# Attention and expert layer on one core: ten instead of eight tiles of the shared expert in the output stage

## What is computed

```python
gate = xt @ Wr + br
_, ids = top_k(gate + gate_bias, 2)            # 2 of 7 experts for each row
probs = softmax(masked)                        # over the chosen two
u = xt @ Wup[e] + bup[e]
g = silu(u @ Wgate[e] + bgate[e]) * u
eo = g @ Wdown[e] + bdown[e]
out = sum over the two experts of probs * eo
su = xt @ Wsu + bsu                            # the shared expert, for every row
sg = silu(su @ Wsg + bsg) * su
out = out + sg @ Wsd + bsd
```

## Time and profile of the kernel before

| | |
|---|---|
| median of three runs | 996.62 us |
| profiled execution | 995.83 us |
| its span in the profile | 994.2 us |
| TensorE matmul busy | 907.2 us, 91% |
| VectorE busy | 650.5 us, 65% |
| GpSimd busy | 623.7 us, 63% |
| ScalarE busy | 459.7 us, 46% |
| output stage to expert loop | about 430 us to 562 us to 926 us |
| last stage | 926.5 to 994.2 us |

### The profile page before, as it was taken

How to read it: one execution, slowest core, us unless ns; L and a number is a source line. 1 busy time by engine, 2 the same in 40 slices (tenths; PEclk the granted TensorE clock), 3 DMA queues, 4 the chain that set the end, 5 groups by cost and what they waited for, 6 DMA issues and landing times. The chain is left out here.

```text
span 994.2 us, 17086 instructions
## 1 busy us (share of the span) xinstructions
PE 907.2 (91%) x5047; PEld 405.8 (41%) x5048; DVE 650.5 (65%) x1019; ACT 459.7 (46%) x846; POOL 623.7 (63%) x565
## 2 busy tenths in 40 slices
PE   2889895799998999989999589999999999999898
PEld 1345442122221222246644245555555555555443
DVE  7788777598887888367775155544555555543388
ACT  3376655688887888722353022332333233223540
POOL 6465556367777775533127398988989999700372
PEclk9788998599999999999999799999999999999999
DMA  7234635444454532133426755656555656535666
GB/s 223 86 97 117 181 107 160 140 159 169 168 177 161 175 106 68 53 108 128 163 102 228 279 165 185 196 183 190 192 181 194 202 178 195 160 110 185 235 194 229
DMA packets 106059, 162.26 MB, mean 163 GB/s; under 512 B 12536, under 2 KB 55608, under 8 KB 105616
## 3 DMA queue, kind: packets, MB, share of 16 engines
q1 hardware_dynamic: 93056, 116.38, 36.5%
q0 software_dynamic: 12896, 45.10, 13.5%
q10 hardware_dynamic: 48, 0.05, 0.0%
HBM read 107.88 MB, written 53.48 MB: 162 GB/s over the span
## 5 line engine op out<-in xcount | busy, mean ns | idle before, releaser
L1089 ACT ACTIVATE p_t<-a_psT 128x512 f32<-128x512 f32 x256 | 138.9, 595 | 47.8 <-PE a_psT L1212 46.5
L1136 DVE TENSOR_REDUCE nm<-quad 128x4 bf16<-128x1984 f32 x60 | 133.9, 2231 | 35.8 <-PE quad L1197 35.8
L1906 ACT ACTIVATE e_xT<-quad 128x512 f16<-128x512 f32 x38 | 22.7, 597 | 230.8 <-PE quad L1970 230.8
L1039 POOL TENSOR_TENSOR p_sum<-p_t,p_t 128x512 f32<-128x512 f32 x64 | 81.2, 1277 | 50.1 <-ACT p_t L1089 49.8
L1980 PE MATMUL quad<-w_exp,e_xT 128*128 x456 | 106.3, 383 | 4.5 <-issue 2.3
L1980 PE MATMUL e_psY<-w_exp,e_gT 128*128 x456 | 104.6, 379 | 0.0
L1980 PE MATMUL quad<-w_exp,e_uT 128*128 x456 | 104.6, 379 | 0.0
L1212 PE MATMUL a_psT<-q_stk,k_stk 98*128 98x512 f16 x256 | 84.2, 399 | 11.7 <-ACT p_t L1089 9.4
L215 POOL TENSOR_TENSOR w_exp<-e_raw,w_exp 128x1024 f32 (+1 forms) x42 | 90.9, 2165 | 6.0 <-POOL e_raw L212 4.5
L207 POOL TENSOR_TENSOR w_exp<-e_raw,ws_tile 128x1024 f32 (+1 forms) x42 | 80.3, 1911 | 6.4 <-DMA e_raw<-in_L_ffn_Wup_dram 5.5
L1937 DVE SCALAR_TENSOR_TENSOR e_g<-quad,bias 128x512 f32<-128x512 f32 x38 | 26.3, 692 | 84.1 <-PE e_psGT L1970 79.0
(11 more groups left out here) (340 smaller groups left out, 1778.7 us busy)
## 6 DMA issues: line engine op xcount, KB each, us to landing
xs_dram<-zero SPq DMA_DIRECT2D x38, 256.0 KB, 7.0
e_x<-xs_dram SPq DMA_DIRECT2D x38, 256.0 KB, 3.1
bias<-in_L_ffn_bup_dram SPq DMA_DIRECT2D x38, 256.0 KB, 3.3
bias<-in_L_ffn_bgate_dram SPq DMA_DIRECT2D x38, 256.0 KB, 3.4
ys_dram<-e_y SPq DMA_DIRECT2D x38, 256.0 KB, 2.0
q_dram<-q_st SPq DMA_DIRECT2D x24, 256.0 KB, 3.1
k_dram<-k_st SPq DMA_DIRECT2D x24, 256.0 KB, 3.8
q_stk<-q_dram SPq DMA_DIRECT2D x64, 96.0 KB
```

The costliest lines, as they stand in the source:

```text
L1039: pool.tensor_tensor(p_sum[:, w % SUMS, :], probs(w, 0), probs(w, 1), ALU.add).then_inc(s["sum_1"], 1)
L1089: act.activation(probs(w, k), psT[:, k % 2], ACT.Exp, scale=SCALE / (QS * QS)).then_inc(s["exp"], 1)
L1136: dve.tensor_reduce(nm[:, i, :, 0:1].rearrange("p h o -> p (h o)"), psS[:, :, 0:NMAIN], AX.X, ALU.max, negate=True)
```

## The change

- `NFIRST` is 10. In `output` the shared expert has three groups of 512, 512 and 256 tokens; a 256-token group works on 256 columns. Buffers are laid out anew.
- In `late` six tiles are left, in a group of 512 tokens (tiles 12 to 15) and one of 256 (tiles 10 and 11). The order of the tiles is 0 to 9, 12 to 15, 10, 11, for gathers, totals and stores. There are ten bias products instead of eight.
- ScalarE, when it is through with its work in `output`, waits for the scatters and the output projection and fetches the rows of the first two blocks. The two loads at the start of `routed` go. The wait of SyncE for the landing of the `y` stores moves from the end of `output` to the end of `routed`.
- `split_half`: the first piece is a `tensor_scalar` instead of a `tensor_tensor` with the broadcast scale; both kinds of `seen` products go. GpSimd's loop over experts is written out.

```diff
-NFIRST = 8
+NFIRST = 10
...
             if piece == 0:
                 pool.wait_ge(loaded, 16 * arrived)
-                pool.tensor_tensor(hi, w, ws, ALU.mult).then_inc(w_scaled, 1)
+                pool.tensor_scalar(hi, w, WS, 0.0, ALU.mult, ALU.add).then_inc(w_scaled, 1)
             elif piece == 1:
                 pool.wait_ge(w_scaled, 2 * n + 1)
-
-                pool.tensor_tensor(seen[:, :], ws_tile[:, :], ws_tile[:, :], ALU.add)
                 pool.tensor_scalar(w, w, WS, 0.0, ALU.mult, ALU.add).then_inc(w_scaled, 1)
...
@@ output, SyncE @@
-            for q in y_st:
-                sp.wait_ge(q, 8 * NFIRST)
...
@@ output, ScalarE, at its end @@
+            for landed in scattered:
+                act.wait_ge(landed, 16 * TOP * NT // IN_FLIGHT)
+            act.wait_ge(s["y_mm"], NT)
+            for k in range(2):
+                act.dma_start(g_["rows_in"][:, k], g_["xs_dram"][k * P:(k + 1) * P, :]).then_inc(g_["rows_loaded"][k], 16)
...
@@ output, VectorE, after the probabilities @@
-            for j in range(TB):
-                down(0, j)
-            for j in range(TB):
-                down(1, j)
+            for c in range(KD):
+                gated(2, c)
+                if c:
+                    gated_low(2, c - 1)
+                down(0, c)
+            gated_low(2, KD - 1)
+            for grp in (1, 2):
+                for j in range(WIDTH[grp] // P):
+                    down(grp, j)
...
@@ routed, SyncE @@
+                    for q in g_["shared_stored"]:
+                        sp.wait_ge(q, 8 * NFIRST)
                     sp.dma_start(g_["of_first"][:, :, :], g_["x1_dram"][0:NBASE * P, :].rearrange("(n p) d -> p n d", p=P)).then_inc(late_ld, 16)
-            load(0, 0)
             bias_row(0, 0, "L0_ffn_bup", "b_up", "u_r")
-            load(1, 1)
...
@@ routed, GpSimd @@
-            with pool.Fori(E_EARLY, E - 1) as k:
+            for k in range(E_EARLY, E + 1):
                 halves(k, False)
-            halves(E - 1, False)
-
-            halves(E, False)
...
@@ late @@
+    SPAN = ((1, slice(0, S), NT - TB), (0, slice(NFIRST * P - 2 * S, S), NFIRST))
+    WIDTH = [at.stop - at.start for _, at, _ in SPAN]
+    TILES = list(range(NFIRST)) + list(range(NT - TB, NT)) + list(range(NFIRST, NT - TB))
...
             gated_low(1, KD - 1)
+            for j in range(2):
+                gathered(2 * TB + j)
+                first_total(TB + j)
             for j in range(TB):
                 gathered(NFIRST + j)
-                first_total(TB + j)
                 down(0, j)
-            for j in range(TB):
+                first_total(TB + 2 + j)
+            for j in range(NT - TB - NFIRST):
                 gathered(NFIRST + TB + j)
                 down(1, j)
```

More of the change, by code:

```diff
@@ L186, in build @@
         w_scaled = sem("w_scaled")
+        rows_loaded = [sem(f"e_x_loaded{k}") for k in range(2)]
+        shared_stored = [sem(f"o_y_stored{k}") for k in range(2)]
         mine.clear()
@@ L1384, in nth_chunk @@
         def nth_chunk(kind, grp, c):
-            return KD * ORDER.index((kind, grp)) + c
+            return CHUNKS.index((kind, grp, c))
         def chunk_bank(kind, grp, c):
@@ L1651, in _ @@
             for c in range(KD):
+                up_low(2, c)
+            for c in range(KD):
                 gated(0, c)
@@ L1737, in up @@
                 at = slice(c * P, (c + 1) * P)
-                product(chunk_bank("u", grp, c), [(weight(0, y, q)[:, at], xT_all[:, grp, q, x, :]) for q in range(KD)
+                product(chunk_bank("u", grp, c)[:, 0:WIDTH[grp]], [(weight(0, y, q)[:, at], xT_all[:, grp, q, x, 0:WIDTH[grp]]) for q in range(KD)
                                                   for x, y in ((0, 0), (1, 0), (0, 1))]).then_inc(s["u_mm"], 1)
@@ L1744, in gate @@
                 at = slice(c * P, (c + 1) * P)
-                product(chunk_bank("g", grp, c), [(weight(1, y, q)[:, at], uT[grp][:, q, x, :]) for q in range(KD)
+                product(chunk_bank("g", grp, c)[:, 0:WIDTH[grp]], [(weight(1, y, q)[:, at], uT[grp][:, q, x, :]) for q in range(KD)
                                                   for x, y in ((0, 0), (1, 0), (0, 1))]).then_inc(s["g_mm"], 1)
@@ L1776, in _ @@
             prefix()
[L1777 to L1782, removed]
-            for j in range(TB):
-                down(0, j)
-            for j in range(TB):
-                down(1, j)
+            for grp in (1, 2):
+                for c in range(KD):
+                    up(grp, c)
+            for grp in GROUPS:
+                for c in range(KD):
+                    gate(grp, c)
+            for grp in GROUPS:
+                for j in range(WIDTH[grp] // P):
+                    down(grp, j)
 def routed(nc, t, sem, g_):
@@ L1795, in routed @@
     sb = Map(nc, SBUF_LO + E * g_["PER_E"], g_["AUX_AT"])
-    x_in = sb(tag + "x", [P, 2, D], F32)
+    x_in = g_["rows_in"]
     xT = sb(tag + "xT", [P, 2, 2, KD, P], F16)
@@ L2267, in up @@
                 at = slice(c * P, (c + 1) * P)
-                product(chunk_bank("u", grp, c), [(weight(0, y, q)[:, at], xT[:, grp, q, x, :]) for q in range(KD)
+                product(chunk_bank("u", grp, c)[:, 0:WIDTH[grp]], [(weight(0, y, q)[:, at], xT[:, SPAN[grp][0], q, x, SPAN[grp][1]]) for q in range(KD)
                                                   for x, y in ((0, 0), (1, 0), (0, 1))]).then_inc(s["u_mm"], 1)
@@ L2274, in gate @@
                 at = slice(c * P, (c + 1) * P)
-                product(chunk_bank("g", grp, c), [(weight(1, y, q)[:, at], uT[:, grp, q, x, :]) for q in range(KD)
+                product(chunk_bank("g", grp, c)[:, 0:WIDTH[grp]], [(weight(1, y, q)[:, at], uT[:, grp, q, x, 0:WIDTH[grp]]) for q in range(KD)
                                                   for x, y in ((0, 0), (1, 0), (0, 1))]).then_inc(s["g_mm"], 1)
```

133 lines of the change are left out of this document (70 added, 63 removed).

## The result

Seven runs of the changed kernel have a median of 1002.14 us (1001.16 to 1003.46), seven of the kernel before on the same chip 997.62 us (996.19 to 1000.29). The ratio is 1.0041, interval 1.0026 to 1.0056: slower by about 4 us, 0.4%. The forecast was +3.3 us and 999.9 us, with a range of 996.4 to 1003.5.

What follows compares the result with a forecast made beforehand. TensorE was taken to lead before the change, with VectorE and GpSimd nearly full behind it in the last stage. Loop start +9.6 and last stage -6.3 gave +3.3 us on 996.62, so 999.9 us, range 996.4 to 1003.5.

Steps and rivals of the forecast that it cites:

- the signs named ahead: Restart about 575, block pitch 9.08, last split before 850; last stage 59 us, TensorE hole some 7 us, VectorE without gap.
- Part 1, two tiles: Output stage: two more tiles cost TensorE 15.6 us (upper end 19.1), with 256-column matmuls at 0.108 us and nothing hiding it.
- Part 2, the hand-over: Output stage to expert loop: TensorE's hole 3.4 us instead of 8.7, the loop starting 9.6 us later (6.3 to 13.7).
- I take 2.2 us, the row of this very boundary: Barrier after the output stage: priced at 2.2 us within the new hole, with 0.4 kept for the range.
- The landing of the stores: End of the output stage: SyncE's wait for y to land, 2.0 us, goes from the path.
- The clock's 0.6 us: TensorE's restart in the expert loop: less clock lost after the shorter hole, 0.6 us gained (0 to 2.1).
- Part 3, GpSimd: Weight splitting beside the expert loop: cheaper scaling and the written-out loop gain no time, since GpSimd has 62.5 us of slack.
- Part 4, the last stage: Last stage: TensorE loses 15.6 us of work, but VectorE ends at 985.4, so only 6.3 us come back (3.3 to 10.5).
- Both agree: Last stage: the end from VectorE's work, 985.4, and from the last gather's landing plus products and total, 984.9, taken as agreeing.
- A cheap hand-over: Rival at the hand-over: barrier 0.4 us, no clock lost, loop 6.3 us later; change 0.0, 996.6 us; chance 0.14.
- DMA as the bound: Rival in the last stage: busy DMA lands the last gather 3 us later; +5.4 us, 1002.0 us; chance 0.12.
- TensorE as the leader: Rival in the last stage: TensorE goes on leading, all 15.6 us come back; -6.0 us, 990.6 us; chance 0.10.

Runs made afterwards that it cites:

- both late edits: Changed kernel with up to four tiles' gathers in flight rather than two, and bias products 2 to 4 behind the last group's gates: 997.85 us, ratio 0.9992.

## Why the prediction was right

The sign, the size (+3.3 against +4.1 us) and the main mechanism held. Two terms were off by 1.5 and 2.3 us, in opposite directions, so part of the closeness of the sum is luck. Of the signs named ahead, one did not come: VectorE was not without a gap until the end, and the last stage took 61.2 us for 59.

**Part 1, two tiles: right.** 15.65 us for 15.6. The half-width pitch is 0.109 us in a stream for 0.108. The 512-column products of the same stage are 0.216 us apart (24 from 548.93 to 554.11), as in the text, so half the columns took half the time. Nothing beside the tiles fell behind.

**Part 2, the hand-over: too dear by 1.5 us.** The forecast had a hole of 3.4 us and a loop start 9.6 us later. The hole was 1.7 us and the start 8.1 us later (15.65 - 7.57). The step that failed is "I take 2.2 us, the row of this very boundary". That row was GpSimd's DRAIN of 2.67 us behind its scatters, and the same text had already noted that the new end of TensorE covers the scatters by 17 us. The landing of the stores, 2.0 us in the text as what is left of 4.17, was over at 559.9 on SyncE's queue, so it took 1.7 us. The ten tiles with the old hand-over show 0.2 us at the barrier. The clock's 0.6 us (2.1 us lost behind the old hole, by the 1.12 and 4.39 us of the earlier trace rows where full clock gave 0.60 and 2.75, less the 1.5 us of the hole before the last stage) held: the restart is 8.6 us later, the last stage 8.1.

**Part 3, GpSimd: right.** 1068 ns a piece, last split at 813 us, no change of time in the run of that part alone.

**Part 4, the last stage: right in kind, 4.0 us given back for 6.3.** Hole and half-width operations of VectorE (0.34 us apart) came as said. The 2.3 us are three pieces. VectorE came to the first gathered tile at 949.50, where the forecast, moved with the stage's start, had 948.67: 0.8. Its waits behind that were 0.57 + 1.14 + 2.50 + 0.23 + 0.72 = 5.2 us for 4.2: 1.0. Three errors hide in that: the early waits for gathers were 1.7 us for 3.0, those for the gates 2.7 for 1.2, and the last wait, 0.72 us for a gather, was not in the sum at all. The rest, 0.5, is not traced; short gaps between operations are the likely place. The wait for the gates came out long because the text let TensorE come back from its hole at full clock. It came back at a granted clock of 0.50 (971.65 to 974.40): twelve half-width products took 2.56 us instead of 1.31.

**"Both agree" hid the point.** The forecast's second check, from the gathers, gave 984.9 for VectorE's 985.4, and I took that as support. It was a second bound of the same height. It measured as the first did: last issue 53.3 us after the stage's start for 51.6, landing 5.6 us later for 4.6, and 2.3 us of products and total behind it, 61.2 us. That is why the experiments with one of the two relieved gained 1.6 to 2.3 us, and with both 9.5.

**The rivals.** A cheap hand-over had the right barrier (0.4 us for 0.2 measured), but needed a clock without loss. DMA as the bound had the right suspect in the gathers, but for the wrong reason: it was the limit of two tiles in flight. TensorE as the leader fell by its hole. With a hole of 1.7 us and 4.0 us back from the last stage, the forecast's own sum would have been +7.9 - 4.0 = +3.9 us.

## What to carry to other kernels

Moving work from a stage to an earlier one that the same engine bounds gains nothing by itself: it costs its full price there, 15.6 us here, and gives back only what the next engine allows, 4.0 us. Add up every engine's work and every pacing limit of the stage that is relieved; where two come out alike, relieving one is worth little. And ask of a barrier's row who came last to it, and when that engine's closing DRAIN began: its price moves with that engine, 0.2, 2.2 and 3.7 us at the same barrier here.

## What the runs showed of the hardware

- The barrier behind the output stage had little price of its own: SyncE stood 0.2 us at it in all nine profiles with ten tiles, where the other engines were done before it. The 2.2 us with eight tiles (the kernel before, and with GpSimd's part alone), the 3.3 (with the hand-over alone), and the 3.7 and 4.2 us (with both, with two and with four tiles' gathers in flight) were GpSimd's DRAIN, and the time until it could begin. This DRAIN took 2.67 us behind the scatters in all fourteen profiles, with eight tiles and with ten.
- The granted clock fell with the long holes, and with the short one not always. In the changed kernel, after 1.7 us without work, four transposes still took 0.63 us, at 1.00. Behind 1.8 us more without work the clock was at 0.50, and before 583 it was back at 1.00. In the kernel with the bias products behind the gates the same two holes stood there, 1.71 and 1.79 us, and the product behind them took 2.76 us for 4.11, at 1.00 (576.7 to 579.4). After 5.8 to 8.7 us the same transposes took 1.08 to 1.12 us, at 0.50. In the last stage the stretch of the 6.23 us hole was granted 0.50, and the one with three holes of 1.42, 0.88 and 0.88 us in its place 0.95, by the windows below, of the changed kernel and of the one with both late edits. But there too it fell, behind the third hole: it was 0.50 from 973 to 975, against what the expectation had, and the twelve products from 973.35 took 3.84 us, where the twelve from 977.46 took 2.75 at 1.00.

```profile
967.60:972.60 5.00, 1.35 (x6) 0.88 (x7) 4.73 (x9) 1.54 (x4) 3.83 (x4) 0.50 0.64 169
```

```profile
967.60:972.60 5.00, 1.82 (x12) 0.89 (x11) 4.96 (x11) 1.98 (x6) 3.83 (x4) 0.95 0.75 200
```

- With four tiles in flight GpSimd issues a gather every 1.25 to 1.78 us. They then landed 4.9 us after issue in the median, rather than 4.3 with two tiles in flight, and the 32 of them were out 10.7 us earlier.
